# A graph transformer layer on one core: the gate scatters split around the row scatters, and the decay steps moved behind the last tile

## The reference

```python
q = _l2norm(_silu(h @ Wq).reshape(Bs, Ls, H, DK))
k = _l2norm(_silu(h @ Wk).reshape(Bs, Ls, H, DK))
v = _silu(h @ Wv).reshape(Bs, Ls, H, DV)
beta = jax.nn.sigmoid(h @ Wb)
g = -jnp.exp(A_log) * jax.nn.softplus((h @ Wa).astype(jnp.float32) + dt_bias)
def step(S, x):
    qt, kt, vt, bt, gt = x
    S = S * jnp.exp(gt)[..., None, None]
    kv = jnp.einsum('bhk,ebhkv->ebhv', kt, S)
    delta = (vt[None] - kv) * bt[..., None]
    S = S + kt[None, :, :, :, None] * delta[..., None, :]
    ot = jnp.einsum('bhk,ebhkv->ebhv', qt * scale, S)
    return (S, ot)
core = jnp.einsum('ble,eblhv->blhv', w_full, o)
gate = _silu((h @ Wg).reshape(Bs, Ls, H, DV))
```

## Time and profile before

| | |
|---|---|
| median of 3 runs | 995.51 us (986.03 to 998.89) |
| profiled execution, its time | 995.51 us |
| its span | 993.7 us |
| mean granted clock of PE | 0.985 |
| PE busy | 894.7 us, 90% |
| DVE, POOL, ACT busy | 600.3, 369.8, 254.6 us |

### The profile page before, as it was taken

The page is one execution under the profiler, slowest core; times in us unless marked ns, Lnnn a source line. Parts: engine busy times, 40 slices in busy tenths (PEclk is TensorE's granted clock), DMA queues, the critical chain, the costliest instruction groups (busy, mean ns, idle before and its releaser), DMA issues.

```text
span 993.7 us, 28569 instructions
## 1 busy us (share of the span) xinstructions
PE 894.7 (90%) x12598; PEld 577.6 (58%) x12598; DVE 600.3 (60%) x1288; ACT 254.6 (26%) x502; POOL 369.8 (37%) x303
## 2 busy tenths in 40 slices
PE   3999999999998999999999888888888888888598
PEld 1454453445665444444444478788788788887343
DVE  7799999958884323236075555545555555554274
ACT  1121112201221000032122244333333343333331
POOL 5021100000111200002899576564565646542582
PEclk9999999999999999999999999999999999999989
DMA  8300000120000600000166843433434334321452
GB/s 258 121 1 1 1 1 1 43 63 1 1 2 3 231 1 1 0 1 2 16 244 258 275 124 99 124 105 94 117 99 120 99 101 118 99 57 35 116 145 65
DMA packets 74869, 80.59 MB, mean 81 GB/s; under 512 B 34437, under 2 KB 57655, under 8 KB 74743
## 3 DMA queue, kind: packets, MB, share of 16 engines
q1 hardware_dynamic: 69623, 57.58, 21.1%
q0 software_dynamic: 5120, 21.14, 6.0%
HBM read 54.25 MB, written 24.39 MB: 79 GB/s over the span
## 4 chain that ended last, share of the span: by engine, by line
PE 68%; POOL 11%; DVE 9%; issue 8%; DMA 1%; ACT 1%; SPq 0%; DVEq 0%; POOLq 0%
PE bank L829 16%; PE bank L760 9%; PE bank L530 7%; PE bank L563 4%; PE bank L549 3%; POOL nrm L1274 3%; POOL qkv_slots L1279 2%; PE bank L751 2%; DVE rows L1570 2%; PE bank L930 2%; PE bank L1003 2%; PE bank L919 2%; POOL gb_slots L1269 2%; PE bank L906 2%; PE bank L944 2%
## 5 line engine op out<-in xcount | busy, mean ns | idle before, releaser
L751 PE MATMUL bank<-W,xT 128*128 128x512 f32 x296 | 128.3, 593 | 0.0
L751 PEld LDWEIGHTS bank<-W,xT 128*128 128x128 f32 x296 | 56.0, 190 | 69.9 <-issue 69.7
L829 PE MATMUL bank<-big 64*64 64x64 f32 x2240 | 84.6, 222 | 6.4 <-issue 5.5
L760 PE MATMUL bank<-hs,big 125*125 125x512 f32 x200 | 86.6, 593 | 0.0
L829 PEld LDWEIGHTS bank<-big 64*64 64x64 f32 x2240 | 75.9, 137 | 8.2 <-issue 7.2
L530 PE MATMUL bank<-W,xT 128*125 128x512 f32 x160 | 79.3, 615 | 0.0
L1255 POOL TENSOR_TENSOR big<-big,ident_sb 125x125 f32<-125x125 f32 x10 | 11.4, 1141 | 173.9 <-ACT big L1066 173.9
L829 PE MATMUL bank<-tB 64*64 64x64 f16 x2560 | 59.5, 195 | 16.8 <-issue 12.2
L1314 POOL TENSOR_TENSOR tB<-tA,masks_sb 128x512 f16<-128x512 f16 x20 | 39.3, 1967 | 92.8 <-DVE tA L1816 92.8
L1831 DVE TENSOR_TENSOR tB<-bank,masks_sb 128x512 f16<-128x512 f32 x80 | 54.7, 684 | 21.2 <-PE bank L829 21.1
L760 PEld LDWEIGHTS bank<-hs,big 125*125 125x125 f32 x200 | 37.3, 188 | 47.7 <-issue 47.5
(11 more groups left out here) (302 smaller groups left out, 1874.1 us busy)
## 6 DMA issues: line engine op xcount, KB each, us to landing
big<-qkv_slots SPq DMA_DIRECT2D x40, 256.0 KB, 3.6
rows<-step_rows SPq DMA_DIRECT2D x40, 128.0 KB, 3.5
rows<-gam_rows SPq DMA_DIRECT2D x40, 128.0 KB, 3.3
big<-qkv_slots SPq DMA_DIRECT2D x80, 64.0 KB, 2.7
big<-qkv_slots SPq DMA_DIRECT2D x40, 128.0 KB, 3.0
o_slots<-big SPq DMA_DIRECT2D x40, 128.0 KB, 2.5
x_all<-in_x SPq DMA_DIRECT2D x10, 224.0 KB
out<-tC SPq DMA_DIRECT2D x10, 224.0 KB
```

Of the source, the lines that this page charges most:

```text
L751: last = mm(bank[:, b0, :], xT[:, k, t * P:t * P + 128], W[:, w, k, :], start=(k == 0), stop=(k == KC - 1))
L760: last = mm(bank[0:P, t % 2, :], cnt[:, s, t * P:(t + 1) * P], hs[:, s, :], start=(s == 0), stop=(s == NT - 1))
L829: last = mm(bank[q, b0, a * CL:(a + 1) * CL], lhsT[q, a, :], rhs[q, a, :], start=True, stop=True)
```

## The change: splitting the gate scatters and moving the decay steps

POOL no longer scatters the gates of all ten tiles before the first inverse norm. It scatters those of tiles 0 to 3, and then those of one more tile in each of the first six rounds of the loop over tiles. `gates_in` moves on DVE from behind tile 2 to behind tile 7. `decay_sums` on PE and `decays` on ACT move from behind the q, k, v of tile 7 to behind the output gate of tile 1, that is behind the q, k, v of all tiles; `decay_rows` on DVE moves from behind tile 7 to behind tile 9. No instruction is added or dropped, and the program of SP is the same.

```diff
-GAMMA_AT = 2
-DECAY_AT = 7
+GB_FIRST = 4
+GAMMA_AT = 7
...
@@ PE
                 for w in range(3):
                     project_rows(t, w)
-                if t == DECAY_AT:
-                    decay_sums()
             project_rows(1, 3)
+            decay_sums()
             for t in range(2, LATE):
                 project_rows(t, 3)
...
@@ ACT
                 for w in range(3):
                     feature_rows(t, w)
-                if t == DECAY_AT:
-                    decays()
             feature_rows(1, 3)
+            decays()
             for t in range(2, LATE):
                 feature_rows(t, 3)
...
@@ POOL
-            for t in range(NT):
+            for t in range(GB_FIRST):
                 gates_out(t)
             inverse_norm(0)
             for t in range(NT):
+                if t + GB_FIRST < NT:
+                    gates_out(t + GB_FIRST)
                 if t + 1 < NT:
                     inverse_norm(t + 1)
                 rows_out(t)
...
@@ DVE
                 unit_rows(t)
                 if t == GAMMA_AT:
                     gates_in()
-                if t == DECAY_AT:
-                    decay_rows()
+            decay_rows()
```

## The result

The changed kernel takes 1004.8 us (median of 4 runs, 1003.58 to 1008.35) against 993.65 for the kernel before (4 runs, 986.03 to 998.89): a ratio of 1.0118, with a 95% interval of 1.0074 to 1.0165. It is slower by about 1%; timed again on another chip, beside other kernels, the ratio was 1.0095 (1.0063 to 1.0127). The forecast was 3.5 us and not 10 to 11, and 1004.8 lies outside the stated range of 990 to 1004.

The account below looks back on a forecast made before the run. PE's projections hide everything feeding unit 0 until about 562.5, so at most 0.3 us can be won; SP's late list adds 1.8, stores 1.3, q and k 0.4: 995.5 + 3.5 = 999.0 us, range 990 to 1004.

Parts of the forecast that it names:

- the 9.6 us of slack: SP's idle time between its broadcast loads and the scatters' end, 549.80 to 559.42; forecast more than used up by 11.4.
- Late gates: Rival: the `gbp` load gets no turn among row scatters, DVE stalls at `gates_in`; 1001.5 mild (0.06), 1015.5 full (0.04).
- Within 2%: Whole kernel: change stays inside about 20 us, the least a measurement can tell; same 0.96, slower 0.03, faster 0.01.
- the clock: Rival, chance 0.11: PE's gap grows to 4.4 us, units 0 and 1 run at half clock, 2.5 us more, 1001.5.
- the landing of the stores: Decay stores on SP's queue land later beside four row scatters: 1.3 us taken, bounds nothing to 3.7.
- q and k behind the broadcast loads: Last loads on SP's list follow eight broadcast loads instead of an empty queue: 0.4 us taken, from nothing to 1.9.
- POOL's sum: POOL's gate scatters and inverse norms end within 1 us of before; the `decay_rows` scan behind them shifts SP's list 11.4 us.
- nothing lost: Rival, chance 0.11: SP's list shrinks as broadcast loads no longer meet scatters, q and k asked for at 559.4: 995.5.
- DVE's path: `decay_matrix(0)` and seven `gate_rows` ahead of `lower(0)` end at 567.3 to 569.4, even with PE's path; up to 2 us more.

Follow-up runs that it names:

- q and k first: Changed kernel, with unit 0's q and k loads issued ahead of the wait for the decay stores and the broadcast loads: ratio 1.0077, 999.93 us.
- the fill: Changed kernel plus 36 matmuls of zeros on PE behind the last projection, in its 8.9 us idle gap: ratio 1.0023, plain median 995.61 against 991.66 us.
- the short one: Changed kernel, decay steps behind tile 8, q and k before the second broadcast loads: ratio 1.0027; with nine zero matmuls in PE's gap 0.9947, plain median 989.18 us.

## Why the prediction was wrong

**The way it goes was right.** SP's list, not POOL, carried the loss: the 9.6 us of slack were used up, the wait for the scatters is gone, the loads of q and k come last, PE's projections end where they did, `gates_in` waits for nothing, and the move of the decay steps alone has nearly all of it. Late gates did not happen. "Within 2%" held. Wrong was the size: 3.5 us against 10.9 in the trace and 10 to 11 in time. The steps that failed are four terms that were each taken too small: the clock, left out of the sum (2.9 in the trace), the landing of the stores (3.1 for 1.3), q and k behind the broadcast loads (2.2 for 0.4), and POOL's sum (13.1 for 11.4). The terms, by their steps:

- *POOL's sum.* "Eight gate scatters end at 474.09 + 0.96": 474.09 is the start of the seventh. The eighth ends 1.3 us later, and one inverse norm took 3.72 again beside DVE's product. The scan of `decay_rows` ended 13.1 us later than before and not 11.4: 1.7 us missed.
- *Stores beside the scatters.* "I take 1.3", with an upper bound of 3.7. It was 3.1 (5.9 against 2.8). **This is a step that failed by its choice:** the rows taken were loads, though the trace before had these very stores beside two scatters (3.7 to 4.3 us to landing), and the value was taken in the lower half of the stated bounds. The last store and the last scatter landed within 0.3 us of each other, and the four stores take 3.4 us in all when nothing is queued beside them. The Trainium skill, page "DMA: Bandwidth & Descriptors", section "Queues, rings and completion order", has the engines take turns between queues packet by packet. The forecast worked out from it that all four stores land no sooner than the scatters; the trace agrees for the last one alone, for the other three landed 3.9 to 6.5 us ahead of the last scatter.
- *The eight broadcast loads* were 1.0 us faster than before, 5.2 and not 6.2, as the rival "nothing lost" said.
- *q and k behind the broadcast loads.* "I take 0.4" of at most 1.9. It was 2.2: 5.6 us from asking to PE's start, 3.4 before, and 3.6 with q and k first (t0 + 94.5 to 98.1).
- These four make the gap: 13.1 + 3.1 - 1.0 - 9.6 + 2.2 = 7.8, measured 8.0.
- *The clock.* It was a rival at 0.11 for a gap of 4.4 us, with a price of 2.5. The gap was 8.9, the clock fell in both profiles, and `lower(2)` is 2.9 later than `features(0)` accounts for: 1.7 up to `lower(0)`, which the fill took away whole, and 1.1 from there to `lower(2)`, which is the clock's only by argument (that way took 23.9 us before, 25.1 and 24.9 in the changed kernel, 24.5 with PE filled, and 26.6 in the kernel before with five matmuls of fill). The fill gave 2.8 back against the first profile and 2.1 against the second. The price was right as far as the traces tell, and its place in the sum wrong: it hangs on the other terms, so they should not have stood as separate cases. Each term a little larger would have drawn in the next.
- *DVE's path* came out even with PE's by the forecast. In the changed kernel it is 3.8 us ahead of it, since q and k came later still; with q and k first it became the last wait, as said.
- *The range* took its lower end from the scatter of single runs, and its upper end from the mechanisms alone; the upper bounds of the sum (7.4) plus the clock reach 1005.4, and a scatter of runs on top of that was left out.

## What to carry to other kernels

Where a small result goes through HBM and back before a stage can start, the slack is that of the whole list on its queue, and it shrinks when the list is moved into a stretch in which another queue is full: the last small store may then land with the big ones, and the list waits for the last. Price each transfer by a row that has the same neighbours, and where none has, take the end of the other queue's backlog roughly as the upper bound of its landing. A gap that grows on TensorE must be priced with the clock behind it, where TensorE is in the chain; where another engine was the busy one, the low clock here cost nothing that could be measured. And when one late input is repaired, look at which other input is late for the same reason.

## What the runs showed of the hardware

- Four stores of 160 KB in all took 9.4 us from first issue to landing beside four queued row scatters of 786 KB each, and 3.4 us alone; their issuing itself stretched from 2.1 to 3.5. Of the nine, 7.4 are the last store's own landing; the other three took 2.7 to 4.3, and 1.7 to 1.9 with nothing beside them.
- Eight broadcast loads took 5.2 us to issue with the row scatters gone and 9.7 in the middle of them: SP's issuing took longer beside the traffic of another queue.
- The granted clock fell to 0.50 near t0 + 99.5 in the profiles with PE gaps of 8.9, 3.1, 2.3 and 1.6 us ahead of unit 0; in the last two PE had taken up work again by then, at t0 + 98.8 and 98.1. Behind the gap of 0.9 us, and where zeros filled the gap, it stayed at 1.00 for 9 us or more. In each of these profiles it fell once more, or for the first time, within the first units.
- Nine to 36 matmuls of zeros in the gap were worth 2.8 to 3.1 us at `lower(2)` in the trace, but nearer to 6 us in time for the long gap (10.1 to 4.0) and 3 for the short one (1.9 to -1.0, on two chips, with about 3 us of uncertainty each). They also shift the later falls of the clock: five in the kernel before moved the next one from t0 + 110 to 106.
